# Fourth layer's attention: two heads' maxima in one operation, on other PSUM banks, with their parts made on three engines and loaded in four transfers

## The reference

```python
qkv = (x @ Wqkv).reshape(b, l, 3, H, HD)
q, k, v = [jnp.moveaxis(qkv[:, :, i], 1, 2) for i in range(3)]
attn = jax.nn.softmax(jnp.einsum('bhqd,bhkd->bhqk', q, k) * HD ** (-0.5), axis=-1)
out = jnp.einsum('bhqk,bhkd->bhqd', attn, v)
out = jnp.moveaxis(out, 1, 2).reshape(b, l, d)
return out @ Wout * jax.nn.sigmoid(x @ Wgate)
```

## Time and profile before

| | us |
|---|---|
| median of 3 runs | 960.28 (958.65 to 960.83) |
| profiled execution, its own time | 963.37 |
| its span in the trace | 962.1 |
| TensorE matmuls busy | 696.2 (72%) |
| VectorE busy | 589.9 (61%) |
| ScalarE busy | 395.6 (41%) |
| GpSimd busy | 285.3 (30%) |

### The profile page before, as it was taken

One profiled execution on the slowest core, in us unless ns is written; L12 is line 12 of the kernel. 1 busy time (PEld: TensorE's weight loads), 2 busy tenths in 40 slices (PEclk: granted clock), 3 DMA queues, 4 the chain that ended last, 5 costly groups with the idle time before them and its releaser, 6 DMA issues. The chain is left out here.

```text
span 962.1 us, 14376 instructions
## 1 busy us (share of the span) xinstructions
PE 696.2 (72%) x4255; PEld 518.5 (54%) x4255; DVE 589.9 (61%) x1621; ACT 395.6 (41%) x952; POOL 285.3 (30%) x300
## 2 busy tenths in 40 slices
PE   4889967752788379229986797989964429979980
PEld 3889834642667358228865474656543215546550
DVE  5665568528688612386667556879844328864944
ACT  3101324433744223135443335767761114446652
POOL 2243134440000164300000002445411754453551
PEclk9999958856699779668997798999985759998995
DMA  9991001211100150318007321222100212214214
GB/s 281 228 289 51 1 19 46 57 46 31 44 1 1 9 47 8 102 60 350 1 1 186 104 61 33 73 73 72 48 3 22 64 48 57 62 47 140 75 56 134
DMA packets 79561, 72.90 MB, mean 76 GB/s; under 512 B 9617, under 2 KB 73884, under 8 KB 78976
## 3 DMA queue, kind: packets, MB, share of 16 engines
q1 hardware_dynamic: 58880, 53.41, 20.1%
q0 software_dynamic: 7072, 12.38, 5.2%
q10 hardware_dynamic: 13536, 6.21, 2.7%
HBM read 42.83 MB, written 27.42 MB: 73 GB/s over the span
## 5 line engine op out<-in xcount | busy, mean ns | idle before, releaser
L1069 POOL DMA_INDIRECT ys<-work,back_to x101 | 101.2, 1002 | 115.9 <-issue 52.2
L2656 DVE TENSOR_REDUCE work<-banks 128x2 f32<-128x512 f32 x128 | 83.2, 681 | 15.6 <-PE banks L2647 14.8
L995 PE MATMUL banks<-weights,work 128*128 x156 | 88.6, 653 | 1.6 <-issue 1.6
L978 PEld LDWEIGHTS banks<-consts,work 128*128 128x128 f32 x156 | 18.8, 147 | 90.6 <-issue 54.3
L978 PE MATMUL banks<-consts,work 128*128 128x128 f32 x156 | 33.7, 299 | 35.2 <-DVE work L3357 15.2
L2647 PE MATMUL banks<-work 96*128 96x256 bf16 x256 | 49.7, 279 | 8.1 <-DVE work L2656 4.8
L988 PE MATMUL banks<-weights,work 128*128 x312 | 52.7, 293 | 2.6 <-issue 2.3
L789 POOL DMA_INDIRECT xs<-t,idx x48 | 49.2, 1025 | 14.8 <-issue 14.0
L1349 POOL DMA_INDIRECT g<-rows,back_to x16 | 15.3, 958 | 122.5 <-DVE back_to L2067 117.9
L3060 PE MATMUL banks<-work 99*128 99x256 bf16 x256 | 48.9, 277 | 0.9 <-issue 0.9
L988 PEld LDWEIGHTS banks<-weights,work 128*128 128x128 f32 x312 | 42.9, 199 | 5.0 <-issue 3.8
(11 more groups left out here) (497 smaller groups left out, 1914.0 us busy)
## 6 DMA issues: line engine op xcount, KB each, us to landing
weights<-in_w SPq DMA_DIRECT2D x1, 6668.0 KB, 19.6
xs<-zero SPq DMA_DIRECT2D x2, 2580.0 KB, 31.7
work<-xs ACTq DMA_DIRECT2D x78, 64.5 KB
weights<-in_w SPq DMA_DIRECT2D x1, 4569.5 KB, 33.3
weights<-in_r SPq DMA_DIRECT2D x1, 2950.5 KB, 26.2
weights<-in_w SPq DMA_DIRECT2D x1, 2124.5 KB, 12.2
ys<-zero SPq DMA_DIRECT2D x1, 2048.0 KB, 27.7
g<-ys SPq DMA_DIRECT2D x8, 256.0 KB, 3.3
```

The source lines that it names most:

```text
L978: ins = pe.transpose(bank(mb + m % 4)[:, 128 * f:128 * f + 128], self.ha[m % 4][:, f * 128:(f + 1) * 128], self.c["ident"])
L995: pe.matmul(bank(mb + n % 4, F), self.hT[n % 4], self.w1[:, bass.ds(off[n] * (F // 128), F)], start=True, stop=True).then_inc(*self.prod1. ...
L1069: g.indirect_dma_start(self.ys[:, :], bass.IndirectOffsetOnAxis(ap=self.n.back_to[:, k:k + 1], axis=0), self.answer(n), None, bounds_check ...
L2656: v.tensor_reduce(self.mxb[:, 2 * h:2 * h + 2], self.n.bank(bank).rearrange("p (r n) -> p r n", r=2), AX, ALU.max, negate=True).then_inc(* ...
```

## The change

- **Maxima of two heads in one operation.** VectorE reduces 128 x 1024 columns, two neighbouring banks, in one instruction. Pass 1 goes to banks 0 to 3, and waits once for each pair of heads, for the maxima of two pairs before.
- **18 heads ahead.** Pass 1 of head s+18 stands in step s; `FirstMaxima` does 18 heads. The maxima are turned after step 8i+7, one step earlier.
- **Banks.** Pass 2 has banks 4 and 5 and waits for the exponential of two heads before. The values' products have bank 6 alone, which the projection now shares; bank 7 holds what bank 5 held. ScalarE copies each quarter (256 columns) instead of each half, after the exponential of head 4j+6.
- **Parts of the maxima.** High part on ScalarE, rest on VectorE, middle and low on GpSimd. SyncE waits for each part before its copy.
- **Nine products instead of six.** The q transfer repeats each of 24 rows three times over 72 partitions; three k transfers put the same 24 rows there three times. The stores of k interleave the parts. `FILLED` is 72.
- The `free` list waits for the low part and for the maxima of the ninth pair. GpSimd's order has the two operations and the values' cast at other places.

```diff
-PAIRS_Q, PAIRS_K = (0, 0, 0, 1, 1, 2), (0, 1, 2, 0, 1, 0)
...
-    ROWS, FILLED = 96, 48
+    ROWS, FILLED, AHEAD = 96, 72, 18
...
-        cols = slice(half * self.HALF, (half + 1) * self.HALF)
-        for x, side, dst in ((0, PAIRS_Q, self.qs[b % 2]), (1, PAIRS_K, self.ks[b % 2])):
-            at = 0
-            for k in (3, 2, 1):
-                first = 8 * side[at]
-                if x == 0:
-                    src = n.parts[0][first:first + 8, b, cols].unsqueeze(0).broadcast_to((k, 8, self.HALF))
-                else:
-                    src = n.parts[1][0:8 * k, b, cols]
-                sp.dma_start(dst[8 * at:8 * (at + k), cols], src).then_inc(*self.heads_in[b % 2][half].up())
-                at += k
+        cols, got = slice(half * self.HALF, (half + 1) * self.HALF), self.heads_in[b % 2][half]
+        q, k = (n.parts[x][0:24, b, cols] for x in range(2))
+        sp.dma_start(self.qs[b % 2][0:72, cols], q.unsqueeze(1).broadcast_to((24, 3, self.HALF))).then_inc(*got.up())
+        for i in range(3):
+            sp.dma_start(self.ks[b % 2][24 * i:24 * i + 24, cols], k).then_inc(*got.up())
...
-        v.wait_ge(*self.pass1.at(s))
-        v.tensor_reduce(self.mxb[:, 2 * h:2 * h + 2], self.n.bank(bank).rearrange("p (r n) -> p r n", r=2), AX, ALU.max,
+        v.wait_ge(*self.pass1.at(s + 1))
+        v.tensor_reduce(self.mxb[:, 2 * h:2 * h + 4], self.n.bank(bank, 1024).rearrange("p (r n) -> p r n", r=4), AX, ALU.max,
                         negate=True).then_inc(*self.mx.up())
...
+    def act_maxima(self, b, half, bank):
+        a = self.scalar
         if b:
-            v.wait_ge(*self.max_loaded(b - 1, half))
-        v.wait_ge(*self.mx_t.at(2 * b + half))
-        v.tensor_copy(mp[:, 0, :], m).then_inc(*D.up())
-        v.wait_ge(*D.now())
-        v.tensor_tensor(self.resid, m, mp[:, 0, :], ALU.subtract).then_inc(*D.up())
-        v.wait_ge(*D.now())
-        v.tensor_copy(mp[:, 1, :], self.resid).then_inc(*D.up())
-        v.wait_ge(*D.now())
-        v.tensor_tensor(mp[:, 2, :], self.resid, mp[:, 1, :], ALU.subtract).then_inc(*self.mp.up())
+            a.wait_ge(*self.max_loaded(b - 1, half))
+        a.wait_ge(*self.mx_t.at(2 * b + half))
+        a.activation(self.mparts[half][:, 0, :], self.n.bank(bank)[0:16, 0:128], ACT.Copy).then_inc(*self.hi.up())
...
-            if s < 112:
-                h.pe_pass1(s + 16, s % 2)
+            p = s + h.AHEAD
+            if p < 128:
+                if p % 2 == 0:
+                    pe.wait_ge(*h.mx.at(p // 2 - 2))
+                h.pe_pass1(p, p % 4)
             if s < 128:
-                q, k, ps = h.qs[b % 2], h.ks[b % 2], bank(2 + s % 3)
+                q, k, ps = h.qs[b % 2], h.ks[b % 2], bank(4 + s % 2)
...
-                if s >= 3:
-                    pe.wait_ge(*h.exp.at(s - 3))
+                if s >= 2:
+                    pe.wait_ge(*h.exp.at(s - 2))
...
-                pe.wait_ge(*h.oT.at(2 * mb + half))
+                pe.wait_ge(*h.oT.at(4 * mb + 2 * half + 1))
...
                 pe.wait_ge(*h.otT.at(m // 16))
+                pe.wait_ge(*h.oT.at(min(4 * (m // 16 + 1), 31)))
...
-            m = s - 2
-            if m >= 0 and m % 8 == 7 and m < 128:
-                mb, half = m // 16, m % 16 // 8
+            if s % 8 == 7 and s < 112:
+                h.act_maxima(s // 16 + 1, s % 16 // 8, 7)
+            m = s - 3
+            if m >= 0 and m % 4 == 3 and m < 128:
+                mb, g4 = m // 16, m % 16 // 4
+                part = slice((g4 % 2) * NS, (g4 % 2 + 1) * NS)
                 if mb:
-                    a.wait_ge(*h.o_t.at(2 * (mb - 1) + half))
-                a.wait_ge(*h.pv.at(4 * mb + 2 * half + 1))
-                a.activation(h.oTb[half], bank(6 + half), ACT.Copy).then_inc(*h.oT.up())
+                    a.wait_ge(*h.o_t.at(2 * (mb - 1) + g4 // 2))
+                a.wait_ge(*h.pv.at(m // 4))
+                a.activation(h.oTb[g4 // 2][:, part], bank(6)[:, part], ACT.Copy).then_inc(*h.oT.up())
```

More of the change, by code:

```diff
@@ L2660, in pe_maxima @@
         pe = self.tensor
[L2661 to L2679 removed]
+        pe.wait_ge(*self.mx.at((16 * b + 8 * half + 7) // 2))
@@ new lines, in dve_maxima, with pool_maxima @@
+    def dve_maxima(self, b, half, bank):
+        v, k = self.vector, 2 * b + half
+        if k:
+            v.wait_ge(*self.low.at(k - 1))
+        v.wait_ge(*self.hi.at(k))
+        v.tensor_tensor(self.resid, self.n.bank(bank)[0:16, 0:128], self.mparts[half][:, 0, :], ALU.subtract).then_inc(*self.rest.up())
+    def pool_maxima(self, b, half):
+        g, k, mp = self.gpsimd, 2 * b + half, self.mparts[half]
+        g.wait_ge(*self.rest.at(k))
+        g.tensor_copy(mp[:, 1, :], self.resid).then_inc(*self.mid.up())
+        g.wait_ge(*self.mid.at(k))
+        g.tensor_tensor(mp[:, 2, :], self.resid, mp[:, 1, :], ALU.subtract).then_inc(*self.low.up())
@@ L2681, in sp_maxima @@
     def sp_maxima(self, b, half):
         sp = self.sync
-        sp.wait_ge(*self.mp.at(2 * b + half))
-        for q in range(3):
+        for q, part in enumerate((self.hi, self.mid, self.low)):
             r = self.ROWS + q
+            sp.wait_ge(*part.at(2 * b + half))
             sp.dma_start(self.qs[b % 2][r:r + 1, half * self.HALF:(half + 1) * self.HALF],
@@ L2822, in pe, with act @@
             yield
+    def act(self):
+        for k in range(12):
+            if k in (5, 9):
+                self.n.heads.act_maxima(0, k // 8, 3)
+            yield
     def dve(self):
@@ L2826, in dve, with pool @@
         for k in range(12):
-            if 0 < k < 9:
-                for s in (2 * k - 2, 2 * k - 1):
-                    h.dve_pass1(s, 6 + s % 2)
+            if 0 < k <= h.AHEAD // 2:
+                h.dve_pass1(2 * k - 2, 6)
             if k in (6, 10):
                 h.dve_maxima(0, k // 8, 3)
+            yield
+    def pool(self):
+        for half in range(2):
+            self.n.heads.pool_maxima(0, half)
             yield
@@ L3186, in pool @@
         values(0)
-        values(1)
         for w in range(8):
             some(1)
+            if w:
+                h.pool_maxima(w, 1)
+            if w < 7:
+                values(w + 1)
             if w >= 2:
                 blend.rows(w - 2)
-            some(4)
+            some(2)
+            if w < 7:
+                h.pool_maxima(w + 1, 0)
+            some(2)
             blend.base(w)
-            if w < 6:
-                values(w + 2)
         blend.rows(6)
@@ L3504, in layer3 @@
     softmax.sent, softmax.norms = sent3, norms
-    softmax.free = [gates.rows.at(3), gates.g.at(3), parts.values.at(3), parts.low.at(7), n.heads.mp.at(1)] + [n.heads.put_done(u) for u in (5, 6, 7)]
+    softmax.free = [gates.rows.at(3), gates.g.at(3), parts.values.at(3), parts.low.at(7), n.heads.low.at(1), n.heads.mx.at(8)] + [n.heads.put_done(u) for u in (5, 6, 7)]
     blend = Blend(n, norms)
```

71 lines of the change are left out of this document (41 added, 30 removed).

## The result

| | before | after |
|---|---|---|
| median of 20 runs each, us | 963.58 (956.46 to 973.18) | 967.34 (959.40 to 974.58) |
| ratio of the times | | 1.0059, 95% interval 1.0034 to 1.0084 |
| profiled execution, its own time | 963.37 | 959.40 |

By the ratio the change makes the kernel slower by 0.6%, some 6 us; the two medians are 3.8 us apart; forecast were 8.2. The profiled execution of the changed kernel is the fastest of its 20 runs. Matched instruction by instruction, it stands 6.7 us earlier than the one of before at 500 us already, ahead of everything that the change touches, and 5.1 us earlier at 505; it gains another 4.8 after 713 us, where nothing was changed. So the two profiles are compared stretch by stretch, each from an instruction that both have.

The account below looks back on a forecast made before the run. TensorE was taken to bound the attention stage. The terms -2.7 + 0.6 + 1.5 + 0 + 7.2 + 1.6 = +8.2 us gave 971.6 us for the profiled execution and 968.5 for the median; range 956 to 980.

Parts of the forecast that it names:

- The wait for the copy: Attention samples: TensorE's turn of the outputs (L3111) waits 0.80 us twice per sample for ScalarE's later copy, L3124 0.7 once.
- three releasers: Attention before the change: TensorE waits for VectorE's maxima, 6.6 and 3.9 us, and the parts' load, 2.2; 12.7 us winnable.
- The 13.3 us of work and the 15.0 us of a sample: Attention before the change: TensorE's work per sample without waits, and the average of five samples; about 1.7 us is waiting.
- The six samples, +7.2: Middle of the fourth layer's attention: each sample takes 16.2 us against 15.0, +1.2, over six samples +7.2 us.
- The first sample, 0: First attention sample: begins with the clock low and the load unhurried, so no change, 0 us.
- The last sample, +1.6: Last attention sample: no first pass or maxima, so nothing won, and two waits for the copy in full, +1.6 us.
- The loads, -2.7: Loads of parts ahead of ScalarE's wait for stores: a half issues in about 1.75 us, two halves save 2.7 us.
- Start of the load against its use, 0: Attention stage: load-to-use time shrinks from 8 to about 6.4 us, but the better spread load still arrives in time, 0 us.
- The rival of the late load: Attention stage: 12 loads come late at 1.0 us each, +12 us, giving 980; chance 0.10.
- The stage boundary, +1.5 and +0.6 before it: Attention start: two more heads, a pair's reduction and GpSimd's operations cost +1.5 us; before it, pass 1 waiting for pairs, +0.6.
- The split is worth nothing here: Parts of the maxima on three engines: VectorE sheds three of four small operations, none on TensorE's path; worth nothing.
- the rival "faster": Attention: deeper banks win if copies finish within 0.66 us of the third head's matmul; named waits vanish, 947 us; chance 0.13.

## Why the prediction was right, point by point

**Direction, size and place: right.** 8.2 us were forecast; by stretches it is +5.9 (3.9 won before, 1.8 lost in the first maxima, 7.8 in the stage, 0.2 right behind it), and the ratio says 0.59% +- 0.25, which is 5.7 us. The times themselves were met less well than they seem. The median of 967.34 is near the 968.5 forecast partly by luck: the base of 960.28 was of three runs, and with 20 it is 963.58, so a base too low made up for a sum too high. The profiled execution was to take 971.6 us and took 959.40; it was 5.1 us ahead at 505 us already and gained 4.8 after 713, where nothing was changed.

**The wait for the copy: right.** 1.46 us from the second pass to the turn were worked out, 1.41 measured; 0.80 lost, 0.74 measured; 16 waits foreseen, 16 found, and 7 at L3124 instead of 8. A sample was to take 16.2 us and takes 16.2. Moving the copy alone gave 13.4 us back, so this is shown and not only argued. It is more than the 8 us that the stage had lost, but it is not the banks' gain alone. The stage of before takes 126.0 and 125.6 us in its two traces, with the new loads and the old banks 120.5, and with all of the change and the copies a head earlier 119.5.

**"The waits view names three releasers": one was left out.** The longest such row of before was the fourth, TensorE's wait at L3089 for ScalarE's copy, 7.5 us at the weight load and 4.8 at the matmul. TensorE already waited for the copy at 8 of the 16 turns, so "all that this change can win here" was more than the 12.7 us named. The 13.3 us of work and the 15.0 us of a sample, from which the sum was made, are not touched by it.

**The six samples, +7.2: too large; it is 97.59 - 92.5 = +5.1.** The step that failed is "against 15.0 us: +1.2, over six samples +7.2". I left the sample with ScalarE's stop of 2.4 us out of the average and then charged six samples, as if that stop came again. It did not: the longest of the six is 16.45. Set against the whole 92.5 us, the same 16.2 would have given +4.7. The second pair of traces, of two other chips, has 97.62 against 90.66 us, +7.0; the samples of after are the same in both, those of before are not.

**The first sample, 0: wrong in this pair of traces.** It takes 16.47 against 15.44 us from start to start, +1.0. It is at half clock for longer (granted clock 0.79 in the row above, 0.89 in the same stretch of before), and it waits for the copies like every other. In the traces of the other chips it is 15.20 in after and 16.87 in before, so that this +1.0 may not be the change's.

**The last sample, +1.6: right.** From its start to the last projection 19.3 us (712.20 - 692.90), against 17.6 before (711.63 - 694.04): +1.7.

**The loads, -2.7: right in kind, too small.** One transfer of q over 72 rows takes 0.82 us of issue, not 0.7, and the three of k 1.34, not 1.05, so 2.2 us for a half against the 1.75 forecast. Two halves took 4.5 us and not 3.5, 1.7 less than before instead of 2.7. At ScalarE's wait 2.2 us were won, counted from the landing of the stores before: 1.7 by the issues and 0.5 since these stores land faster (3.60 us in the chain of after, 4.10 in the earlier trace rows).

```profile
536.75 3.60 DMA k_parts<-xT
540.37 0.53 ACT xT L2739
```

Behind it came 1.4 us more, forecast as "up to 1.7" and not put into the sum: TensorE had been idle for 2.60 instead of 4.84 us and did its next 15 matmuls at full clock. With 0.3 earlier on these make the 3.9 us. So the sum's -2.7 was too small because it left the clock out, and its issue part was too large.

**Start of the load against its use, 0: right, and the new form is why.** 0.4 us of waiting is left in after, where "no row" was to be found; with the old form it is 3.6 us and the stage 5 us longer. The rival of the late load had its mechanism right and its place wrong: with 18 heads ahead TensorE waits 3.3 us for the load once the pace is 14 us per sample.

**The stage boundary, +1.5 and +0.6 before it: the sum right, the cause not.** First maxima and boundary grew by 1.8 us, 2.1 were forecast. But I put 0.4 on GpSimd's two operations, and with VectorE in their place nothing changes: 2.6 us of waiting either way.

**The split is worth nothing here: right**, by two pairs of runs (0.7 us less and 2.7 more without it, neither to be told from zero).

**What the rival "faster" said** is that the copy's wait must not exceed what TensorE has in hand. With the copies a head earlier that comes true as to the wait. It does not as to the price: 13 us under before were its figure, and the kernel stands level with before (0.9998).

## What to carry to other kernels

When a change makes an engine's work cheaper by deeper buffers, look at what had to give up a buffer for it, and count from start to start how long the last producer takes to the consumer that did not move. Here a copy put one head later in an order written by hand cost more than the banks brought, and moving that one line back turned a loss of 1.6% into none; the next bound (the load's 6.4 us) then showed, and only after it the reduction. Try the parts of a change one by one as well: the new loads alone gave 0.5%, and the whole change after all corrections 0.7%, which cannot be told apart. And compare a stretch with the same stretch whole: an average that leaves out a disturbed part must not be multiplied by the number of all parts.

## What was not expected of the hardware

- Two chips ran the same pair of kernels at ratios of 1.0059 (1.0034 to 1.0084) and 1.016 (1.0108 to 1.0213). Intervals within one chip do not cover the difference between chips.
- A reduction of 128 x 1024 from two banks takes 1219 ns, as much as two of 512 back to back (1.20 us by the earlier trace rows): nothing is won on the reduction itself.
- Merging three transfers into one, with the repetition outermost, made the load land 2.2 us later (8.6 against 6.4 us from issue to use, at a DMA share of 0.21 against 0.80), though the queue issued it 0.6 us faster. The median was 14.5 us higher, of which the trace explains little.
